# One key tile in eight squared by ScalarE instead of GpSimd in a two-kernel attention head loop

## The reference

```python
S = jnp.einsum('bhnd,bhmd->bhnm', Q, K) / dh ** 0.5
W_tau = jax.nn.softmax(S, axis=-1)
W_sigma = 1.0 / ((1.0 + jnp.abs(S) / b_) ** 2 + t_ ** 2)
W_sigma = W_sigma / W_sigma.sum(axis=-1, keepdims=True)
tau = jnp.einsum('bhnm,bhmd->bhnd', W_tau, V)
sigma = jnp.einsum('bhnm,bhmd->bhnd', W_sigma, V)
f = 0.5 * tau + 0.5 * sigma
```

## Time and profile before

| what | value |
|---|---|
| median of three runs | 2139.07 us (2138.07 to 2139.43) |
| the profiled execution | 2139.67 us, its span 2137.9 us |
| TensorE matmuls busy | 1622.2 us (76% of the span) |
| VectorE busy | 1888.1 us (88%) |
| ScalarE busy | 1577.8 us (74%) |
| GpSimd busy | 1609.9 us (75%) |
| square L837 | 512 of 1896 ns, 970.9 us |
| adding the constant L813 | 512 of 1124 ns, 575.7 us |
| head loop | from about 99 us to about 1700 us |

### The profile page before, as it was taken

The page is one execution under the profiler, slowest core; times in us unless marked ns, Lnnn a source line. Parts: engine busy times, 40 slices in busy tenths (PEclk is TensorE's granted clock), DMA queues, the critical chain, the costliest instruction groups (busy, mean ns, idle before and its releaser), DMA issues. The chain is left out here.

```text
span 2137.9 us, 34185 instructions
## 1 busy us (share of the span) xinstructions
PE 1622.2 (76%) x8579; PEld 574.7 (27%) x8579; DVE 1888.1 (88%) x3699; ACT 1577.8 (74%) x1395; POOL 1609.9 (75%) x1198
## 2 busy tenths in 40 slices
PE   4477777878777778878777877777777668798976
PEld 2211222212211212222121212112221234366655
DVE  5799999999999999999999999999999378755556
ACT  3288889988888998989898998898998611122243
POOL 2399999999999999999999999999999321100000
PEclk9689999999999999999999999999999878877788
DMA  3300000000000000000000000000000000000001
GB/s 104 103 7 12 12 11 11 15 13 11 11 11 11 15 13 11 11 11 12 14 13 11 11 11 12 14 13 11 11 11 11 1 1 0 1 0 0 0 1 40
DMA packets 28864, 31.75 MB, mean 15 GB/s; under 512 B 5210, under 2 KB 16545, under 8 KB 28833
## 3 DMA queue, kind: packets, MB, share of 16 engines
q1 hardware_dynamic: 28832, 31.40, 4.9%
HBM read 22.74 MB, written 8.39 MB: 15 GB/s over the span
## 5 line engine op out<-in xcount | busy, mean ns | idle before, releaser
L837 POOL TENSOR_TENSOR sigma_weights<-grown 128x1024 f32<-128x1024 f32 x512 | 970.9, 1896 | 0.0
L709 DVE TENSOR_SCALAR sigma_weights<-ps_sig 128x512 int32<-128x512 int32 x1024 | 691.8, 676 | 24.1 <-PE ps_sig L608 19.5
L595 PE MATMUL ps_acc<-tau_weights,v_operand 128*9 128x512 f32 x2048 | 553.3, 620 | 96.1 <-ACT sigma_weights L761 89.4
L789 ACT ACTIVATE tau_weights<-ps_tau 128x1024 f32<-128x1024 f32 x512 | 514.3, 1004 | 149.1 <-PE ps_tau L626 148.7
L608 PE MATMUL ps_sig<-q_operand,k_operand 96*128 96x512 bf16 x1024 | 415.3, 406 | 261.0 <-DVE running_max L716 246.0
L716 DVE TENSOR_TENSOR running_max<-ps_sig,running_max 128x512 f32<-128x512 f32 x896 | 606.8, 677 | 0.0
L813 POOL TENSOR_SCALAR grown<-sigma_weights,shape_operand 128x1024 f32<-128x1024 f32 x512 | 575.7, 1124 | 39.2 <-DVE sigma_weights L709 38.9
L595 PE MATMUL ps_acc<-sigma_weights,v_operand 128*9 128x512 f32 x2048 | 555.3, 622 | 0.2 <-ACT sigma_weights L761 0.2
L755 ACT ACTIVATE sigma_weights<-sigma_weights,shape_operand 128x2048 f32<-128x2048 f32 x256 | 509.9, 1992 | 17.3 <-POOL sigma_weights L837 17.2
L761 ACT ACTIVATE sigma_weights<-sigma_weights 128x2048 f32<-128x2048 f32 x256 | 485.4, 1896 | 0.1
L626 PE MATMUL ps_tau<-q_operand,k_operand 128*128 128x512 bf16 x1024 | 314.9, 389 | 0.2 <-DMA q_operand<-max_rows 0.2
(11 more groups left out here) (171 smaller groups left out, 1489.5 us busy)
## 6 DMA issues: line engine op xcount, KB each, us to landing
q_operand<-q_parts SPq DMA_DIRECT2D x192, 48.0 KB
k_operand<-k_parts SPq DMA_DIRECT2D x64, 144.0 KB
q_parts<-parts SPq DMA_DIRECT2D x12, 256.0 KB, 2.9
k_parts<-parts SPq DMA_DIRECT2D x12, 256.0 KB, 3.0
x_res<-in_L_attn_x SPq DMA_DIRECT2D x4, 512.0 KB, 7.0
q_operand<-max_rows SPq DMA_DIRECT2D x128, 2.0 KB
out<-x_res SPq DMA_DIRECT2D x4, 512.0 KB, 3.2
experts<-in_L_ffn_expert_w SPq DMA_DIRECT2D x1, 512.0 KB
```

The source lines that it names most:

```text
L595: mm = pe.matmul(ps_acc[32 * q:32 * q + COLS, :], vop[:, (slot - 1 + kind) % SLOTS, j, :], weights[:, half * HALF:(half + 1) * HALF], star ...
L709: dve.tensor_scalar(sig[:, tile % SIG_RING, cols].bitcast(I32), ps_sig[:, half, :].bitcast(I32), SIGN_OFF, None, ALU.bitwise_and)\
L789: act.activation(tau[:, (head_slot * TB + of) % TAU_RING, :], ps_tau[:, of % 2, :, :].rearrange("p h q -> p (h q)"), ACT.Exp, scale=float( ...
L837: pool.tensor_tensor(sig[:, tile % SIG_RING, :], t, t, ALU.mult)\
```

## The change

The third key tile of every head (WHOLE = 2) no longer goes through GpSimd. ScalarE takes it at step 6 of the head's stage, between the tau exponential and the exponential of chunk 0, with one activation Square in place, 128x1024, whose bias is the head's first constant: (u + constant) squared. GpSimd leaves out both `grow` and the square of that tile. Its count of squares is seven a head, and the waits on it go through a new function `pooled`. The logarithm of chunk 1 waits for the new semaphore `sqa_ready` as well. The two small copies of GpSimd stay at j = 2; behind them comes grow(3), and the square of tile 3 after grow(4), as before.

```diff
@@ -43,6 +43,8 @@
 TAU_SHIFT = 4
 TAU_RING = 6
 GROWN_RING = 3
+WHOLE = 2
+POOLED = TB - 1
 CHUNK = 2
 SIG_RING = 12
 LOG_LAG, EXP_LAG = 5, 6
@@ -495,6 +497,7 @@
         sig_ready, mag_ready, run_ready = sem("sig_scores_ready"), sem("magnitudes_ready"), sem("running_max_ready")
         grown_ready = sem("grown_ready")
         sqp_ready = sem("pool_squares_ready")
+        sqa_ready = sem("act_squares_ready")
         ln_done, sig_done = sem("logs_ready"), sem("sigma_weights_ready")
         misc_ready, misc_done = sem("misc_ready"), sem("misc_read")
         mrow_ready, mrow_loaded = sem("mrow_ready"), sem("mrow_loaded")
@@ -517,6 +520,12 @@
                     stage(i * SLOTS + k, k % SLOTS, i + k // SLOTS)
             for s in range((LOOPS + 1) * SLOTS, NH + 2):
                 stage(s, s % SLOTS, s // SLOTS)
+
+        def pooled(s, j):
+
+            if j < 0:
+                return pooled(s - 1, j + TB)
+            return s * POOLED + (j - (j > WHOLE))
 
         def at(s, low, high):
 
@@ -751,8 +760,17 @@
             def take_logs(n, slot, c):
 
                 tile = chunk(slot, c)
-                act.wait_ge(sqp_ready, n * TB + (c * CHUNK + CHUNK))
+                act.wait_ge(sqp_ready, pooled(n, c * CHUNK + CHUNK))
+                if c == WHOLE // CHUNK:
+                    act.wait_ge(sqa_ready, n + 1)
                 act.activation(tile, tile, ACT.Ln, bias=shape[:, slot, 1:2]).then_inc(ln_done, 1)
+
+            def square_whole(s, slot):
+
+                act.wait_ge(mag_ready, s * (2 * TB) + (2 * WHOLE + 2))
+                act.wait_ge(sqp_ready, pooled(s, 1))
+                tile = sig[:, (slot * TB + WHOLE) % SIG_RING, :]
+                act.activation(tile, tile, ACT.Square, bias=shape[:, slot, 0:1]).then_inc(sqa_ready, 1)
 
             def invert(n, slot, c):
 
@@ -789,6 +807,8 @@
                         act.activation(tau[:, (head_slot * TB + of) % TAU_RING, :],
                                        ps_tau[:, of % 2, :, :].rearrange("p h q -> p (h q)"),
                                        ACT.Exp, scale=float(DH) ** -0.5).then_inc(tau_done, 1)
+                    if j == WHOLE + LOG_LAG - 1 and at(s, 0, NH - 1):
+                        square_whole(s, slot)
                     lagged(invert, s, slot, j, EXP_LAG)
                     lagged(take_logs, s, slot, j, LOG_LAG)
 
@@ -806,7 +826,7 @@
             def grow(s, slot, j):
 
                 pool.wait_ge(mag_ready, s * (2 * TB) + (2 * j + 2))
-                wait(pool, sqp_ready, s * TB + (j - GROWN_RING + 1))
+                wait(pool, sqp_ready, pooled(s, j - GROWN_RING + 1))
                 alone(pool, w["pool_passed"])
                 tile = slot * TB + j
                 u = sig[:, tile % SIG_RING, :]
@@ -828,11 +848,14 @@
                         if at(s, 0, NH - 2):
                             copy_shape(s + 1, (slot + 1) % SLOTS)
                     if j + 1 < TB:
-                        grow(s, slot, j + 1)
+                        if j + 1 != WHOLE:
+                            grow(s, slot, j + 1)
                     elif at(s, 0, NH - 2):
                         pool.wait_ge(head_copied, s * 2 + 3)
                         grow(s + 1, (slot + 1) % SLOTS, 0)
-                    pool.wait_ge(grown_ready, s * TB + (j + 1))
+                    if j == WHOLE:
+                        continue
+                    pool.wait_ge(grown_ready, pooled(s, j + 1))
                     t = grown[:, tile % GROWN_RING, :]
                     pool.tensor_tensor(sig[:, tile % SIG_RING, :], t, t, ALU.mult)\
                         .then_inc(sqp_ready, 1)
```

## The result

The kernel after takes 2051.81 us in the median (2050.47 to 2053.57, 4 runs), the kernel before beside it 2139.25 us (2138.07 to 2141.16, 4 runs). The ratio is 0.9591, with a 95% interval from 0.9574 to 0.9608. The profiled execution took 2050.47 us, its span is 2048.6 us, 89.3 us shorter than the 2137.9 of before.

The account below looks back on a forecast made before the run. GpSimd was taken to bound the head loop; with ScalarE the longest after, 60 x (24.67 - 23.20) = 88 us came off the profiled 2139.67, less 0.6 for the median: 2050.7 us, range 2039 to 2085.

Parts of the forecast that it names:

- What bounds it before: Head loop: GpSimd sets the pace, 24.03 us a head plus 0.57 idle, against 24.67 measured.
- L687 as a stand: VectorE's 64-column addition, 2.68 us in the mean, mostly waits until GpSimd runs out of ready tiles.
- GpSimd's part: Head loop: one L813 and one L837 removed, 2.96 us, leaving 21.07 us a head and about 2 us idle.
- VectorE's stand: Addition L687 in the head loop: its wait shrinks to 1.3 us, making VectorE's head 22.9 us.
- ScalarE's part: Head loop: the added Square costs 1.05 us, making ScalarE's head 23.20 us, the longest.
- The waits: Head loop: the Square's and logarithm's new waits cost nothing; holds of VectorE only use its spare 0.3 us.
- The clock: TensorE in the head loop: with stands of 1.3 us the granted clock stays up, without dips to half.
- Rival 1: Head loop: L687's stand doesn't shrink (2117 us), or, second half, ScalarE still starves (2099 us); chance 0.16.
- The sum: 60 heads times (24.67 - 23.20) gives 88 us less, nothing counted elsewhere: 2050.7 us.
- Rival 2: ScalarE: each Square brings two table loads, head 25.77 us, 66 us more, 2205 us; chance 0.04.
- Rival 3: Head loop: held by the loop through the rings, not GpSimd; nothing won, within 0.2% of 2139; chance 0.03.
- The lock: SBUF contention of VectorE's L687 with GpSimd: the skill has it wait one instruction; the prediction, mostly until GpSimd runs dry.

Follow-up runs that it names:

- e4: Kernel before without VectorE's addition L687 (heads 1 to 64, only the semaphore raised, result lacks the addition): 2099.39 us, ratio 0.9811.
- e2: Kernel after without ScalarE's Square, tile 2 going into the logarithm as its plain magnitude, all counts and waits kept: 2034.93 us, ratio 0.9508.
- e3: Kernel after without VectorE's addition L696 (heads 1 to 64, only the semaphore raised, result lacks the addition): 2112.47 us, ratio 0.9857.
- e12: On top of e9, tile 2 split in every head: ScalarE squares the second 512 queries, GpSimd the first 512: 2093.15 us, ratio 0.9785.
- e8: Kernel after with two tiles a head on ScalarE (2 and 4, at steps 6 and 7) and six on GpSimd: 2120.47 us, ratio 0.9915.
- e9: Kernel after with VectorE's addition one head later at step 4, and the Square behind the exponential of chunk 0: 2049.51 us, ratio 0.9579.

## Why the prediction was right

**What bounds it before.** Right. GpSimd's 24.03 us a head was confirmed by e4 (24.01), and the reading of L687 as a stand by the same run.

**GpSimd's part.** Right: seven tiles, idle 2.16 us a head where about 2 was forecast.

**VectorE's stand.** Forecast 1.3, measured 1.323 us, and by the step that the sum took: tile 4 is taken up 0.23 us late where "about 0.2" was forecast and 1.69 was read before. It is equal at all heads, as GpSimd's lateness is. Its head, 22.9 by the sum, is 22.94 in e2, where it can be seen alone.

**ScalarE's part.** Forecast 1.05 us to the next instruction and 1.15 long, measured 1.04 and 1.134. Head 23.20, measured 23.20. Idle 0.0 where under 0.3 was forecast.

**The waits.** Right in the result: none shows. VectorE waits 24.1 us for scores in the stretch, 0.40 a head, where in e2, with VectorE as the bound, it idles 1376.3 - 1369.2 = 7.1 us, 0.12 a head. The 0.28 between are the 0.26 that it has to spare, so its holds cost nothing, as forecast.

**The clock.** Right in the outcome (1.00 throughout), by a wrong reason, and so by luck. I took half clock for a result of the long stands, and argued that a stand of 1.3 us is short enough. e4 and e3 have no stand at all, and their mean clocks are 0.95 and 0.94. e3 and the kernel after differ in how TensorE's idle time is divided: the Square ahead of the exponential of chunk 0 made a wait of 1.98 us that the stand happened to split. Had VectorE's addition not been there, the change as made would have given 2112 us and the range would have missed. Rival 1's second half (ScalarE starved) was the real danger, by a way that I had not named.

**The sum.** 88.4 us from the loop against 1480.4 - 1392.2 = 88.2 measured; 0 from elsewhere against 89.3 - 88.2 = 1.1. 2050.7 forecast, 2051.81 measured.

**Rivals.** Rival 1 did not come about: the stand did shrink, and nothing starved. Rival 2 did not: no table load stands by the Square, which the page ScalarE: Activation LUTs of the Trainium skill (Table sets: the hidden batching unit) leaves open for Square and this trace settles. Rival 3 fell with GpSimd's and ScalarE's idle times having changed places.

The lock once more. By the Trainium skill (SBUF — State Buffer, Who interferes with whom) the second to issue is blocked until the first instruction finishes. The rows agree where one instruction is all that is left to GpSimd (after: 1.32 us), and disagree where the next is queued behind it: e12's addition sat through the end of one and the whole of another. Nor does it always wait until GpSimd runs dry; the prediction's "mostly" is right, and no more. Of the 61 additions in the loop before, 36 sat through two to seven instructions and ended where GpSimd then paused for 0.92 us; 25 got in behind the first one, with the next already begun (the 0.63 us one of the earlier trace rows). All 61 end 0.07 to 0.09 us behind the end of a GpSimd instruction. What decides which one stays open.

## What to carry to other kernels

Write down, for each engine, what one turn of the loop costs it start to start, and forecast the turn as the largest of these; here that gave 24.03, 23.20 and 22.94 us where e4, the kernel after and e2 measured 24.01, 23.20 and 22.94. Look at an instruction of varying duration as a wait in disguise and ask what ends it; it belongs where its partner pauses. Don't share work by a mean over turns before a trace shows that what an engine has to spare in one turn reaches the next, and put the moved work behind what another engine waits for, not ahead of it.

## What had not been expected of the hardware

- Less work made the kernel slower: without VectorE's addition 2112 us against 2052, TensorE's clock 0.94 against 1.00 in the mean. Every head had a gap of 1.98 us, and only those with half clock took longer; in the kernel after, gaps of 1.22 and 0.74 us at neighbouring steps left the clock at 1.00.
- The longest gap does not tell whether the clock falls: 45 falls in 60 heads with gaps of at most 1.56 us (e4), 4 with a gap of over 2.5 us in 55 heads (e12).
- The addition of 64 columns takes 0.215 us alone (e8, e9), and 0.35 to 7.26 us beside GpSimd in the kernel before.
- The Square of 128x1024 with a bias column: 1.134 us, 1.04 to the next; of 128x512, 0.61 to the next.
